# Record tables of a graph kernel with their rows permuted inside each batch of 512, so that a partition's four records lie side by side

## The chip, the cores and the metric

The kernel runs on one core of a Trainium2 chip. The metric is the device time of one launch in microseconds (us), the median of three timed runs. A profile is taken in an execution of its own, beside the timed ones; its span is the time from its first instruction to its last.

## The reference, cut to what matters

Four graph layers, each followed by a mixture-of-experts layer, work on a table `x` of 3125 nodes by 256 features and one list of 50000 edges (`src`, `dst`, attributes per edge). What the change touches is how an edge's data are found. Each graph layer has the form of layer 0:

```python
h = x @ W_in2f                                   # nodes
Wij = ssp(rbf @ Wf1 + bf1) @ Wf2 + bf2           # rbf: 64 attributes per edge
Wij = Wij * dist_cut                             # one weight per edge
x_ij = h[idx_j] * Wij                            # row of the node at the far end
m = jax.ops.segment_sum(x_ij, idx_i, num_segments=n_atoms)   # sum at the near end
m = ssp(m @ Wo1 + bo1) @ Wo2 + bo2
return x + m
```

Layer 0 sums at `src`; layers 1 to 3 sum at `dst`. Layer 1 uses 16 attributes per edge and an attention with a softmax over a node's edges, layer 2 no attributes, layer 3 128 attributes and an attention.

## The kernel before

Nodes stand in 25 tiles of 128. So that a sum over a node's edges becomes a matmul with a 0/1 matrix, the kernel first sorts the edges. Every edge gets a slot number; slots are grouped in pairs of tiles (256 slots) that hold edges of one node tile only, and there are 440 tiles of 128 slots (220 pairs). Two tables in device memory hold one record per slot: `records_by_src` (68 numbers, 272 bytes: the 64 attributes of layer 0 and four numbers of placement) and `records_by_dst` (148 numbers, 592 bytes: 128 and 16 attributes and four of placement). `META` is the number of placement columns: a weight, the far node, the near node inside its tile, and a one. A slot without an edge keeps a blank record, whose near node is -1.

**l0n**, the first stage, makes both. Three things run beside each other.

- *The src numbers.* `CellNumbering` (from L524) sorts by src, which is unsorted. The edges stand in a [128, 391] grid; 390 full columns go in 30 groups of 13. For a group, VectorE makes 0/1 tiles (`hot_group`, L653), TensorE counts with them (L818, L820) and VectorE picks each edge's own count out (`take_group`, one instruction per column, L726). Then `put_group` (L738) casts the 13 columns to integers into `to.pos` and raises `pos_ready`. The odd column 391 is cast at L749. After the groups VectorE computes the pairs' tables (25 instructions at L765).
- *The dst numbers.* `Numbering.vector` (L437 to L517) sorts by dst in one go over all 391 columns, also on VectorE, after the node tiles' part of l0n. `pos` is cast at L494; the pairs' tables follow, to the stage's last VectorE instruction, L517.
- *The src scatter.* `Scatter` (from L825) runs on Pool. A ring of record buffers is filled by the SyncE queue from the attributes; `copy` (L872) waits until the group's numbers are out (`placed`, L870), then copies placement and numbers; `scatter` sends one indirect DMA per column (L890), 128 records each to the rows that `pos` names. `scatter_left` does the last columns from `to.pos` itself (L925). The dst table is scattered by the same class in the stage l0e.

The edge stages **l0e** (by src), **l1e** and **l3e** (by dst) each run 110 batches of 512 slots, four tiles of 128. For a batch, the SyncE queue loads the records (`load_batch`, L1105), VectorE casts the far nodes (`find`, L1143), Pool gathers four times 128 rows of the node table (L1121), and the other engines compute and sum. Five record buffers form a ring; `rec_free` lets a buffer be loaded again. Between l0e and l1e, a stage called the means loads 20 numbers (80 bytes) of the dst records, and l1e loads the last four (16 bytes).

`batch_records` gives the view of a batch in the table. Slot number and table row were the same, so slot `t * 128 + p` of a batch lay `t * 128 + p` rows behind the batch's first: a partition p of the record tile took four pieces, one per tile t, 128 rows apart. For a batch that is 512 pieces.

Of the kernel before, what the change touches and what calls it, by code (L numbers as in the profile page):

```python
# [8 lines left out]
I32 = mybir.dt.int32  # L9
# [3 lines left out]
ALU = mybir.AluOpType  # L13
# [3 lines left out]
P = 128  # L17
# [7 lines left out]
EC = E // P  # L25
# [3 lines left out]
BATCH = 4  # L29
# [26 lines left out]
def at(tensor, t, width):  # L56

    if isinstance(t, int):
        return tensor[:, t * width:(t + 1) * width]
    return tensor[:, bass.ds(t * width, width)]  # L60
# [106 lines left out]
def row(vector):  # L167

    return vector.rearrange("(o n) -> o n", o=1)


def column(vector):

    return vector.rearrange("(p o) -> p o", o=1)


def spread(vector):

    return row(vector).to_broadcast([P, vector.shape[0]])
# [7 lines left out]
def tiled(ap, width):  # L187
    return ap.rearrange("p (t d) -> p t d", d=width)
# [210 lines left out]
class Numbering:  # L399
# [37 lines left out]
    def vector(self, dve, net):  # L437
        to, near, far = self.to, self.near, self.far
        t = {n: (v if n == "ps" else v[:, :]) for n, v in self.t.items()}
        part, blk, counted = t["part"], t["blk"], self.t["counted"]  # L440
        match = [t[f"match{k}"] for k in range(UN)]
        link = Chain(dve, self.chain)
# [36 lines left out]
        with dve.Fori(0, NI) as i:  # L479
# [3 lines left out]
            for k in range(UN):  # L483
                b = i * UN + k
# [6 lines left out]
            dve.wait_ge(self.pos_step, base3 + 3 * UN)  # L491
        link(dve.tensor_tensor(pos[0], pos[0], pos[1], ALU.add))
        link(dve.tensor_copy(to.pos[:, :], pos[0]))

        m = to.meta[:, :].rearrange("p (j r) -> p j r", r=META)
        link(dve.memset(to.meta[:, :], 1.0))
# [27 lines left out]
class CellNumbering:  # L524
# [13 lines left out]
    def __init__(self, s, net, shared, to, near, far, weight, spare, turned_into):  # L538
# [23 lines left out]
        self.hot = [s.sb(f"cell_hot{b}", [P, self.COLUMNS * KEYS], BF16) for b in range(2)]  # L562
        self.posf = [s.sb(f"cell_posf{b}", [P, self.COLUMNS]) for b in range(2)]
        self.posf_left = s.sb("cell_posf_left", [P, 1])
        self.picked = [s.sb(f"cell_picked{b}", [P, KEYS]) for b in range(4)]
        self.of_column = s.sb("cell_of_column", [self.ROWS, self.PARTS * CELLS], BF16)
        self.upto_column = s.sb("cell_upto_column", [self.ROWS, self.PARTS * CELLS])
# [89 lines left out]
    def vector(self, dve, net):  # L657
        t, to, near, far = self.t, self.to, self.near, self.far
        key, a_i, b_i = self.key, t["part"], self.part_b
        link = Chain(dve, self.chain)  # L660
# [72 lines left out]
        def put_group(g, b):  # L733
            dve.wait_ge(self.taken, (g + 1) * self.COLUMNS // 2 + 2)
            if (g + 1) * self.COLUMNS % 2:
                dve.wait_ge(self.odd_taken, g // 2 + 1)
            dve.sem_inc(self.tick, 1)
            dve.tensor_copy(at(to.pos, g, self.COLUMNS), self.posf[b][:, :]).then_inc(self.pos_ready, 1)  # L738

        take_group(0, 0)  # L740
        put_group(0, 0)
        for g in range(1, self.GROUPS):
            if g + 1 < self.GROUPS:
                self.hot_group(dve, g + 1, (g + 1) % 2)
            take_group(g, g % 2)
            put_group(g, g % 2)
        link(dve.tensor_tensor_reduce(self.picked[0][:, 0:CELLS], self.hot_left[:, 0:CELLS], self.upto_left[:, :], 1.0, 0.0,
                                      ALU.mult, ALU.add, self.posf_left[:, :]))
        dve.tensor_copy(to.pos[:, EC:EC + 1], self.posf_left[:, :]).then_inc(self.pos_ready, 1)  # L749

        link(dve.memset(self.end[:, NT - 1:NT], float(PAIRS * PAIR - 1)))
        link(dve.tensor_scalar(self.end[:, 0:NT - 1], self.first[:, 1:NT], float(PAIR), -1.0, ALU.mult, ALU.add))
# [192 lines left out]
def batch_records(records, q, lo, hi):  # L945

    rows = records[bass.ds(q * (BATCH * P), BATCH * P), :]
    return rows.rearrange("(t p) r -> p t r", p=P)[:, :, lo:hi]


def l0_gnn_nodes(net):
# [128 lines left out]
class Gather:  # L1080
# [21 lines left out]

    def load_batch(self, sp, q, b):
        sp.wait_ge(self.rec_free, q + 1)
        sp.dma_start(tiled(self.rec[b][:, :], self.n), batch_records(self.placed.records, q, self.lo, self.placed.width))\  # L1105
            .then_inc(self.rec_loaded[b], 16)

    def load(self, sp, more=None):
# [1929 lines left out]
def combine_and_means(net, name, to):  # L3038
# [13 lines left out]
    with ExitStack() as ctx:  # L3052
# [58 lines left out]
        @block.sync  # L3111
        def _(sp):
            def load(q, i, b):
                sp.wait_ge(rest_ready, q + 1)
                sp.dma_start(tiled(rec[b][:, :], n), batch_records(placed.records, q, lo, placed.width))\
                    .then_inc(loaded[b], 16)

            def put(q, i, b):
                sp.wait_ge(kept, RING + q + 1)
                sp.dma_start(net.attr_parts[bass.ds(q * P, P), :], partsT[b][:, :]).then_inc(stored[b], 16)  # L3120

            skewed(sp, (0, by_five(load)), (9, put), ring=DEEP)
            for b in range(DEEP):
                sp.wait_ge(stored[b], NB // DEEP * 16)
# [1311 lines left out]
```

## Time and profile before

| what | us |
|---|---|
| median of the timed runs | 6331.62 |
| the timed runs | 6319.6 to 6334.9 |
| the profiled execution: its span | 7197.4 |
| l0n in it: from 15.8 to | 832 |
| l0e: to | 1957 |
| means | 2541 to 2761 |
| l1e | 2878 to 3994 |
| l3e | 5993 to 6817 |

The stage limits are the first and last instructions of a stage's lines in the trace. The profiled execution is not one of the timed runs; its span stands beside their median because every duration of a single instruction comes from it.

### The profile page before, as it was taken

How to read it: one execution, taken by the hardware profiler on the slowest of the kernel's cores; microseconds unless marked ns; L12 is line 12 of the kernel's file. 1: busy time of each engine (PE TensorE's matmuls, PEld its weight loads, DVE VectorE, ACT ScalarE, POOL GpSimd, SP SyncE). 2: the span in 40 equal slices, each digit the busy share in tenths (PEclk: the TensorE clock that was granted, in tenths of full speed). 3: DMA queues.
4: the chain of work that ended last, by engine and by line, in shares of the span. 5: the costliest groups of instructions: out<-in, count | busy, mean ns of one | idle time of the engine just before them, and what ended most of it. 6: DMA issues, size and time to landing. Idle time of an engine off the chain costs nothing. (4 is left out here: it accounts for less than half of the span.)

```text
span 7197.4 us, 118819 instructions
## 1 busy us (share of the span) xinstructions
PE 5162.2 (72%) x25594; PEld 3845.3 (53%) x25595; DVE 4306.9 (60%) x13225; ACT 2821.1 (39%) x8212; POOL 3018.8 (42%) x3493
## 2 busy tenths in 40 slices
PE   3333377787745657788888399969999996767686
PEld 2222255555533425566666366655657774655575
DVE  4334655666536757799999677773433335655622
ACT  0000255565521143567676311113633333655522
POOL 4665155555444630788888022213310003555421
PEclk9999688888866857899999599989999997777788
DMA  6411133333324752222223255644420003444443
GB/s 215 152 44 38 47 91 88 90 92 95 82 71 139 215 130 63 67 69 67 69 67 67 68 170 182 188 144 136 148 70 9 13 8 100 120 106 110 93 148 124
DMA packets 787071, 719.50 MB, mean 100 GB/s; under 512 B 349384, under 2 KB 692974, under 8 KB 786383
## 3 DMA queue, kind: packets, MB, share of 16 engines
q1 hardware_dynamic: 596344, 372.06, 18.4%
q0 software_dynamic: 120064, 280.26, 14.5%
q10 hardware_dynamic: 70486, 65.22, 2.6%
q8 instruction: 63, 1.03, 0.1%
q14 instruction: 114, 0.93, 0.0%
HBM read 520.74 MB, written 201.60 MB: 100 GB/s over the span
## 5 line engine op out<-in xcount | busy, mean ns | idle before, releaser
L1121 POOL DMA_INDIRECT l3e_rows<-table,l3e_idx x440 | 425.9, 968 | 961.4 <-DVE l3e_idx L1143 600.7
L1121 POOL DMA_INDIRECT l0e_rows<-table,l0e_idx x440 | 425.5, 967 | 580.8 <-DVE l0e_idx L1143 438.6
L1121 POOL DMA_INDIRECT l1e_rows<-table,l1e_idx x440 | 429.6, 976 | 121.4 <-issue 121.4
L3470 ACT ACTIVATE l1e_weighted<-l1e_rows,l1e_power 128x64 f32<-128x64 f32 x1760 | 463.0, 334 | 14.7 <-ACT l1e_power L3461 7.3
L1411 PE MATMUL l0e_ps_w<-l0e_wf,l0e_hidT 128*128 128x256 f32 x1760 | 461.7, 421 | 0.0
L1411 PEld LDWEIGHTS l0e_ps_w<-l0e_wf,l0e_hidT 128*128 128x128 f32 x1760 | 363.4, 212 | 163.7 <-issue 109.3
L890 POOL DMA_INDIRECT records_by_src<-l0n_rec_src,l0n_pos_at_src x390 | 376.3, 965 | 119.2 <-issue 112.3
L818 PE MATMUL l0n_cell_ps<-l0n_cell_hot,l0n_cell_before 128*128 128x175 bf16 x390 | 133.4, 342 | 406.5 <-issue 233.7
L3425 PE MATMUL l3e_ps_s<-l3e_weighted,l3e_onehot 128*128 128x257 f32 x880 | 301.6, 499 | 132.8 <-ACT l3e_weighted L3472 84.6
L3411 PE MATMUL l1e_ps_row<-net_ident,l1e_logit 128*128 128x128 f32 x1760 | 277.7, 281 | 127.1 <-DVE l1e_logit L3606 126.2
L726 DVE CUSTOM_DVE_ANT_0 l0n_cell_picked<-l0n_cell_hot,l0n_cell_ps 128x175 f32<-128x175 bf16 x390 | 114.6, 333 | 394.1 <-remote 310.2
L1402 PE MATMUL l0e_ps_h<-l0e_rbfT,l0e_wf 64*128 64x512 f32 x440 | 163.6, 805 | 256.2 <-ACT l0e_rbfT L1438 195.7
L2144 ACT ACTIVATE l2fe_hT<-l2fe_ps_h,l2fe_own,l2fe_own 128x320 f32<-128x320 f32 x320 | 197.4, 617 | 310.8 <-PE l2fe_ps_h L2094 310.5
L2777 ACT ACTIVATE l1fg_hT<-l1fg_ps_h,l1fg_b_cols 128x256 f32<-128x256 f32 x256 | 107.3, 470 | 530.4 <-PE l1fg_ps_h L2720 511.2
L3425 PEld LDWEIGHTS l3e_ps_s<-l3e_weighted,l3e_onehot 128*128 128x128 f32 x880 | 202.3, 247 | 206.7 <-ACT l3e_weighted L3472 105.5
L3601 POOL TENSOR_TENSOR l1e_e<-l1e_e,l1x_att 128x512 f32<-128x512 f32 x220 | 274.4, 1269 | 89.4 <-DVE l1e_e L3584 53.0
L3411 PEld LDWEIGHTS l1e_ps_row<-net_ident,l1e_logit 128*128 128x128 f32 x1760 | 192.9, 138 | 207.5 <-issue 154.4
L3999 PE MATMUL l2d_ps<-l2d_wide,net_work 128*128 128x512 f32 (+2 forms) x800 | 292.0, 521 | 8.2 <-DVE l2d_wide L4050 5.9
L818 PEld LDWEIGHTS l0n_cell_ps<-l0n_cell_hot,l0n_cell_before 128*128 128x128 bf16 x390 | 50.9, 131 | 450.0 <-issue 252.0
L3328 DVE TENSOR_REDUCE l1e_tile_top<-l1e_ps_row 128x2 f32<-128x512 f32 x440 | 287.7, 684 | 5.8 <-PE l1e_ps_row L3414 4.5
L1343 DVE SCALAR_TENSOR_TENSOR l0e_hidT<-l0e_ps_h,l0e_bf_low,l0e_raised 128x512 f32<-128x512 f32 x220 | 154.9, 746 | 220.9 <-ACT l0e_raised L1457 177.3
L2197 DVE SCALAR_TENSOR_TENSOR net_x<-l2fe_ps_y,l2fe_mix,net_x 128x256 f32 x200 | 96.7, 484 | 309.4 <-PE l2fe_ps_y L2106 309.4
(843 smaller groups left out, 15399.4 us busy)
## 6 DMA issues: line engine op xcount, KB each, us to landing
counts<-l1f_total ACTq DMA_DIRECT2D x272, 128.0 KB
l1fg_w_in<-in_L_ffn_W SPq DMA_DIRECT2D x32, 1024.0 KB
l1fg_w_out<-in_L_ffn_W SPq DMA_DIRECT2D x32, 1024.0 KB
records_by_dst<-l0n_blank_dst SPq DMA_DIRECT2D x5, 6512.0 KB
l3e_rec<-records_by_dst SPq DMA_DIRECT2D x110, 296.0 KB
l2d_counts<-counts SPq DMA_DIRECT2D x208, 128.0 KB, 2.4
l2d_counts<-counts POOLq DMA_DIRECT2D x192, 128.0 KB
l3fg_w_in<-in_L_ffn_w SPq DMA_DIRECT2D x16, 1024.0 KB
```

The source lines that it names most:

```text
L818: pe.matmul(out, self.before[:, :], self.hot[g % 2][:, c * KEYS:c * KEYS + CELLS], start=True, stop=False)
L890: pool.indirect_dma_start(self.to.records, bass.IndirectOffsetOnAxis(self.pos_at[b][:, j:j + 1], 0), at(self.rec[b], j, self.to.width), No ...
L1121: pool.indirect_dma_start(at(self.rows[b], k, self.width), None, self.table, bass.IndirectOffsetOnAxis(self.idx[b][:, k:k + 1], 0)).then_i ...
L1402: pe.matmul(ps_h[:, c, :], wf1[half, :], rbfT[b][half, :], start=True, stop=True).then_inc(hidden, 1)
L1411: ins = pe.matmul(ps_w[:, k, m * D:(m + 1) * D], hidT[b][:, c * WIDE + (2 * k + m) * P:c * WIDE + (2 * k + m + 1) * P], at(wf2, c, D), sta ...
L2144: act.activation(hT[l][:, m * GROUP + half * PART:m * GROUP + (half + 1) * PART], ps_h[:, c % 4, 0:PART], func, bias=own[l][0][:, m:m + 1] ...
L3328: dve.tensor_reduce(tile_top[:, c:c + w], tiled(ps_row[:, side, 0:w * PAIR], PAIR), AX.X, ALU.max)\
L3411: pe.matmul(ps_row[:, side, lo:lo + P], logit[b][:, c:c + 1].to_broadcast([P, P]), net.ident[:, :], is_transpose=True, start=h == h0 and m ...
L3425: ins = pe.matmul(ps_s[:, k, 0:W], at(g.onehot[b], m, P), at(weighted, m, W), start=m == 2 * k, stop=m > 2 * k)
L3470: act.activation(out[:, h, 0:each], g.rows[b][:, lo:lo + each], ACT.Copy, scale=power[b][:, m * heads + h:m * heads + h + 1])
L3601: pool.tensor_tensor(e, e, self.att[:, :].unsqueeze(1).to_broadcast([P, 2, D]), ALU.mult).then_inc(self.times_att, 1)
L3999: ins = pe.matmul(ps[0:k_in, n % 2, 0:width(g)], lhsT, wide[k % WIDE][:, 0:width(g)], start=t == 0, stop=False)
```

## The change

The row of a slot in both record tables is permuted inside each batch of 512 slots. With slot = 512 q + 128 t + p, the row was 512 q + 128 t + p and becomes 512 q + 4 p + t. The four records of partition p are then four rows that follow each other. The slot itself, so the tile and the partition in which an edge is processed, stays.

- `batch_records` reads the new order; where all columns are loaded (l0e by src, l3e by dst, `lo == 0`) a partition takes one piece: 1088 bytes for src, 2368 for dst, 128 pieces a batch. Where only the last columns are loaded (means, l1e) there are still 512 pieces.
- `row_of_slot` is new: eight integer instructions on VectorE, each waiting for the one before, that turn a slot's number into its row. It is called on the 13 columns of each group in `put_group`, on the odd column, and once on the dst table's 391 columns. In `put_group` the cast before it is now waited for as well. After the odd column a wait for all of the row numbers is added.
- Two new tiles, `cell_low` and `cell_high`, [128, 13]; the dst table uses tiles that are there.

```diff
 class Numbering, vector:
+        self.other = self.t["match0"][:, :].bitcast(I32)
         ...
         link(dve.tensor_tensor(pos[0], pos[0], pos[1], ALU.add))
         link(dve.tensor_copy(to.pos[:, :], pos[0]))
+        link(row_of_slot(dve, link, to.pos[:, :], part, self.other))

 class CellNumbering, __init__:
+        self.low = s.sb("cell_low", [P, self.COLUMNS], I32)
+        self.high = s.sb("cell_high", [P, self.COLUMNS], I32)
 put_group:
             dve.sem_inc(self.tick, 1)
-            dve.tensor_copy(at(to.pos, g, self.COLUMNS), self.posf[b][:, :]).then_inc(self.pos_ready, 1)
+            slot = at(to.pos, g, self.COLUMNS)
+            link(dve.tensor_copy(slot, self.posf[b][:, :]))
+            row_of_slot(dve, link, slot, self.low[:, :], self.high[:, :]).then_inc(self.pos_ready, 1)
 the odd column:
-        dve.tensor_copy(to.pos[:, EC:EC + 1], self.posf_left[:, :]).then_inc(self.pos_ready, 1)
+        link(dve.tensor_copy(to.pos[:, EC:EC + 1], self.posf_left[:, :]))
+        row_of_slot(dve, link, to.pos[:, EC:EC + 1], self.low[:, 0:1], self.high[:, 0:1]).then_inc(self.pos_ready, 1)
+        dve.wait_ge(self.pos_ready, self.GROUPS + 1)
+        dve.sem_inc(self.tick, 1)

 def batch_records(records, q, lo, hi):
     rows = records[bass.ds(q * (BATCH * P), BATCH * P), :]
-    return rows.rearrange("(t p) r -> p t r", p=P)[:, :, lo:hi]
+    if (lo, hi) == (0, records.shape[1]):
+        return rows.rearrange("(p t) r -> p (t r)", p=P)
+    return rows.rearrange("(p t) r -> p t r", p=P)[:, :, lo:hi]
+
+def row_of_slot(dve, link, slot, low, high):
+    link(dve.tensor_single_scalar(low, slot, P - 1, op=ALU.bitwise_and))
+    link(dve.tensor_single_scalar(low, low, 2, op=ALU.logical_shift_left))
+    link(dve.tensor_single_scalar(high, slot, 7, op=ALU.logical_shift_right))
+    link(dve.tensor_single_scalar(high, high, BATCH - 1, op=ALU.bitwise_and))
+    link(dve.tensor_tensor(low, low, high, ALU.bitwise_or))
+    link(dve.tensor_single_scalar(high, slot, 9, op=ALU.logical_shift_right))
+    link(dve.tensor_single_scalar(high, high, 9, op=ALU.logical_shift_left))
+    return dve.tensor_tensor(slot, low, high, ALU.bitwise_or)

 Gather.load_batch:
         sp.wait_ge(self.rec_free, q + 1)
-        sp.dma_start(tiled(self.rec[b][:, :], self.n), batch_records(self.placed.records, q, self.lo, self.placed.width))\
+        rec = self.rec[b][:, :] if self.lo == 0 else tiled(self.rec[b][:, :], self.n)
+        sp.dma_start(rec, batch_records(self.placed.records, q, self.lo, self.placed.width))\
             .then_inc(self.rec_loaded[b], 16)
```

## Rows read from the trace of the kernel before

**Rows 1.** The page's head: span and instructions.
```profile
span 7197.4 us, 118819 instructions
```

**Rows 2.** Waits by ended idle time, 0 to 840: total us, count, longest us.
```profile
DVE l0n_cell_picked L726 <- remote: 310.2, 51, 11.3
POOL l0n_rec_src L872 <- DVE l_pos_src L738: 152.5, 14, 55.9
```

**Rows 3.** Timeline, l0n: start, us, engine, line, operation; in brackets idle and releaser.
```profile
304.63 0.35 PE L820 MATMUL l0n_cell_ps<-l0n_cell_upto_low,l0n_cell_ident 65*128 65x175 bf16 x1
313.76 0.34 DVE L726 CUSTOM_DVE_ANT_0 l0n_cell_picked<-l0n_cell_hot,l0n_cell_ps 128x175 f32<-128x175 bf16 x1 [9.90 <-remote]
```

**Rows 4.** Timeline, VectorE in l0n.
```profile
66.62 2.36 DVE L653 TENSOR_SCALAR l0n_cell_hot<-l0n_cell_key_row,l0n_cell_key 128x176 bf16<-128x176 bf16 x13
74.73 2.40 DVE L653 TENSOR_SCALAR l0n_cell_hot<-l0n_cell_key_row,l0n_cell_key 128x176 bf16<-128x176 bf16 x13
...
652.23 0.17 DVE L738 CAST l_pos_src<-l0n_cell_posf 128x13 int32<-128x13 f32 x1
...
830.91 0.39 DVE L517 TENSOR_TENSOR net_keep_dst<-l0n_pair_blk 128x219 f32<-128x219 f32 x1
```

**Rows 5.** Timeline, l0e around 1410 (SPq is SyncE's DMA queue).
```profile
1407.72 1.19 ACT L1438 ACTIVATE l0e_rbfT<-l0e_ps_t 64x512 f32<-64x512 f32 x2 [3.65 <-DMA records_by_src<-l0n_rec_src,l0n_pos_at_src]
...
1418.77 0.38 SPq L1105 DMA_DIRECT2D l0e_rec<-records_by_src  x1
1420.09 0.16 DVE L1143 CAST l0e_idx<-l0e_rec 128x4 int32<-128x4 f32 x1
...
1427.80 0.16 DVE L1143 CAST l0e_idx<-l0e_rec 128x4 int32<-128x4 f32 x1
```

**Rows 6.** Stretches: length, busy PE PEld DVE ACT POOL, clock, DMA share, GB/s.
```profile
832.00:1957.00 1125.00, 855.02 (x3524) 617.19 (x3524) 673.32 (x1327) 648.40 (x1431) 606.90 (x616) 0.86 0.35 89
...
5992.00:6818.00 826.00, 577.37 (x2860) 464.04 (x2860) 496.14 (x2425) 462.92 (x1541) 425.90 (x440) 0.77 0.45 111
```

**Rows 7.** Timeline, l3e around 6400.
```profile
6400.45 0.37 SPq L1105 DMA_DIRECT2D l3e_rec<-records_by_dst  x1
6405.19 0.16 DVE L1143 CAST l3e_idx<-l3e_rec 128x4 int32<-128x4 f32 x1
...
6409.99 0.16 DVE L1143 CAST l3e_idx<-l3e_rec 128x4 int32<-128x4 f32 x1
```

**Rows 8.** Pool in l0n, and VectorE beside it: timeline, and L890 grouped.
```profile
75.00 0.25 POOL L872 COPY l0n_rec_src<-l_meta_src 128x52 f32<-128x52 f32 x1 [55.92 <-DVE l_pos_src L738]
...
686.70 0.91 POOL L925 DMA_INDIRECT records_by_src<-l0n_rec_src,l_pos_src  x1 [0.55 <-POOL l0n_rec_src L919]
...
L890 POOL DMA_INDIRECT records_by_src<-l0n_rec_src,l0n_pos_at_src x390: 954/958/1192, 76.4 to 681.9; - x195
...
656.08 12.05 DVE L765 SCALAR_TENSOR_TENSOR l0n_pair_blk<-l0n_pair_no,l0n_cell_first,l0n_pair_blk 128x220 f32<-128x220 f32 x25
662.00 1.15 POOL L890 DMA_INDIRECT records_by_src<-l0n_rec_src,l0n_pos_at_src  x1 [0.30 <-issue]
```

**Rows 9.** DMA: queue (packets, MB, share) 900:1900, 6000:6800; one load's landing.
```profile
q1 hardware_dynamic: 96960, 25.74, 12.3%
...
q1 hardware_dynamic: 55440, 31.83, 15.6%
...
l2d_counts<-counts SPq DMA_DIRECT2D x208, 128.0 KB, 2.4
```

**Rows 10.** Timeline, VectorE's integer and wide instructions near the end of l0n.
```profile
829.09 0.18 DVE L513 TENSOR_SCALAR net_round_word_dst<-net_round_word_dst 128x44 int32<-128x44 int32 x1
829.31 0.24 DVE L514 TENSOR_TENSOR net_round_word_dst<-net_round_word_dst,net_block_row_dst 128x44 int32<-128x44 int32 x1
...
810.41 0.57 DVE L492 TENSOR_TENSOR l0n_pos_a<-l0n_pos_a,l0n_pos_b 128x391 f32<-128x391 f32 x1 [0.21 <-DVE l0n_pos_a L490]
```

**Rows 11.** Waits, 840 to 1960: total us, count, longest us.
```profile
POOL l0e_rows L1121 <- DVE l0e_idx L1143: 438.6, 66, 156.4
```

## The prediction

> **What bounds the kernel now.** I read the page first: its chain of work names only the last few instructions, so it doesn't say what bounds 7197.4 us [rows 1], and the kernel has to be read stage by stage. The second thing to see stands in the times: the profiled execution's own span is 7197.4 us, the timed runs have a median of 6331.6 us. The profiled execution is 866 us longer than the thing that I have to predict, and before any wait is believed it must be known which idle time belongs to the profiled execution alone.
>
> The three stages that the change touches show it. In l0n (both tables' row numbers are computed, and the src table is scattered) the waits show VectorE idle for 310.2 us in 51 pieces with no releaser that the profile knows ("remote") [rows 2]. One of them: the matmul that VectorE waits for ends at 304.63 + 0.35 = 304.98, VectorE starts at 313.76 [rows 3], while the usual round of 13 columns takes 74.73 - 66.62 = 8.11 us altogether [rows 4]. In l0e, ScalarE idles 3.65 us before its copy and the row names as releaser a scatter of the stage before, long over [rows 5]. An undisturbed batch there takes 1427.80 - 1420.09 = 7.71 us, 110 of them 848 us; the stage has 1125 us [rows 5, 6]: 277 too many. In l3e a batch takes 6409.99 - 6405.19 = 4.80 us, 110 of them 528 us, the stage has 826 us [rows 6, 7]: 298 too many.
>
> What l0n would be without those stalls: VectorE's first row numbers are out at about 75 (Pool's copy of them starts at 75.00 [rows 8]); 29 further groups at 8.11 make 235, so 310; from its last group to its last instruction it took 830.91 + 0.39 - 652.23 = 179 us [rows 4], so it would end at 489. Pool ends its scatter at 686.70 + 0.91 = 687.6 [rows 8]; of its waits for row numbers, 152.5 us in all, only the first, 55.9 us, is before the loop [rows 2], so 96.6 go with VectorE's stalls and it would end at 591. In the profiled execution VectorE ends l0n; without the stalls Pool does, and the stage shrinks by 831 - 591 = 240. The three together: 240 + 277 + 298 = 815 us, of the 866 us that the timed runs lack. So I take it that the timed runs have next to none of these stalls, that Pool's chain of indirect DMAs sets the end of l0n with VectorE about 100 us ahead of it, and that l0e and l3e run at the pace of their undisturbed batches.
>
> A rule speaks against that. The Trainium skill (Runtime: NRT & Kernel Launch, The ~15µs preamble/postamble breakdown) says that a profile's total exceeds the executed time by a gap of about 6.2 us, the same for every kernel. By that rule the stalls would be in the timed runs too. Here the difference is 866 us [rows 1], so the trace and the times don't agree with it; what it would do here is the first rival below.
>
> **The change, part by part.** *The record loads, l0e and l3e.* Each of the 2 x 110 loads becomes 128 pieces instead of 512, with the same bytes. In l0e the hardware queue's packets took 12.3% of 16 engines x 1000 us over 96960 packets, 20 ns each (a mix of 272 B and others); in l3e 15.6% x 16 x 800 us / 55440 = 36 ns for 592 B [rows 9]. One engine has 32 pieces of a load: 0.65 us and 1.15 us. A piece four times as long costs between one old piece and four: the load saves 0 to 0.49 us in l0e, 0 to 0.86 us in l3e, at the engine. Who gets it? A load is issued when a batch's records are released, three steps behind, for the batch five further on, so it is needed at the second find after it. l0e: issued 1418.77, needed 1427.80, 9.0 us. l3e: issued 6400.45, needed 6409.99, 9.5 us [rows 5, 7]. A 128 KB load from the same queue lands in 2.4 us [rows 9]; for l0e's 136 KB that is near; for l3e's 296 KB, by bytes, at most 5.6 us (an estimate from that row). Both are in time with 3.9 us or more to spare, so the gain is hidden: 0. If that cover were gone, it is the second rival.
>
> *The narrow loads (means, l1e).* They still have 512 pieces of 80 and 16 bytes, from other addresses. Nothing in the rows tells their cost apart; I take 0, either sign, a few us.
>
> *Eight integer instructions after each group's row numbers (l0n, src table).* A shift of 44 columns takes 0.18 us and the next instruction of the chain starts 0.22 us after it, a two-input one takes 0.24 [rows 10]; the group's own 13-column cast takes 0.17 [rows 4]. Six at 0.22 and two at 0.28 are 1.9 us a group. Thirty groups are 57 us, the odd column 1.5 us. *The dst table's eight instructions over 391 columns:* the nearest row is 0.57 us [rows 10], so at most 8 x 0.6 = 4.8 us. Together 63 us on VectorE. A group then takes 10.0 us; Pool needs (591 - 75) / 30 = 17 us for one and stays behind. VectorE ends at 489 + 63 = 552, Pool at 591: 39 us remain, hidden. If the cover is gone, it costs 63.
>
> *The first group's row numbers.* Nothing hides these: Pool's first copy waits 55.92 us for them [rows 8] and everything on Pool follows. +1.9 us on the path. Between 0 and 1.9 if the blank rows were late too; I take 1.9.
>
> *Pool beside VectorE's new instructions.* While VectorE runs 25 two-input instructions back to back [rows 8] (12.05 us), Pool's indirect DMA takes 1.15 us instead of its median 0.958: 0.19 more in each 1.45. For 1.9 us of new instructions a group that makes 0.25 us, for 30 groups 7.5 us at most, on Pool, which ends the stage; 0 at least, since six of the eight have one input. I take 3.
>
> The Trainium skill (SBUF — State Buffer, Who interferes with whom) says that VectorE and GpSimd share a port pair as an exclusive lock, so that the second to come is blocked completely for the other's whole instruction. By that Pool would lose up to all of the 59 us of new instructions in the loop; the rows show a fifth of an instruction's time, so by rows it is 3.
>
> *The last wait* (the row numbers' count after the odd column) stops VectorE for one cast's latency, some 0.2 us; behind it are only the instructions that are hidden with it.
>
> *Order of edges:* a slot keeps its tile and partition, so every matmul and segment sees the same data; the scatters write as many rows. 0.
>
> **The sum.** +1.9 + 3 = +5 us on 6331.6: **6336.5 us**, +0.08%. Within 0.3% (19 us, about what a measurement of this kernel can tell from no change).
>
> **The rivals.** *VectorE ends l0n (slower).* If the stalls are in the timed runs as well, VectorE is last in l0n by 831 - 688 = 143 us and the 63 us lie bare: 6331.6 + 63 = 6395. It decides from the point where the stalls that the timed runs keep are over some 59 us of the 310 (39 us of slack, of which Pool keeps pace with 31%). For it: the profile as it stands; 815 is not all of 866, and the undisturbed paces come from single batches. Against it: the 866. The skill's rule on the gap leads here. 0.14.
>
> *The port lock (slower).* Pool is held for the whole of each new instruction: 59 us, 6390. Against it the 1.15 us rows. 0.04.
>
> *The loads are on the path (faster).* Pool waits 438.6 us in l0e for the index cast that needs a load [rows 11]; were that the load and not the stalls, the pieces' time comes back, up to (0.49 + 0.86) x 110 = 148 us, half of it as the middle: 6258. Against it: 9 us between issue and need. 0.09.
>
> *A smaller gain from fewer packets beside the row gathers* over 19 us: 0.03.
>
> *The change doesn't make one piece of a row* (pieces stay short): nothing on the path depends on it, so the time is as forecast.
>
> **How the numbers follow.** Forecast 0.70: 6336.5, with 6318 to 6352 for the unknown small costs and the runs' own spread (6319.6 to 6334.9). Slower 0.14 + 0.04, near 6390 to 6395. Faster 0.09 + 0.03. The range reaches to the slower cases, which hold more: 6314 to 6396, leaving out 0.12.
>
> **What the next profile would show.** The hardware queue's packets fall by 384 a batch in l0e and l3e; the loads land sooner and no stage's undisturbed batch (7.7 and 4.8 us) gets shorter. Pool's first copy starts near 77. VectorE's last l0n instruction comes up to 63 us later. The stalls may move with the number of packets or instructions, so the profiled span can change by more than the median, in either direction, and is not the test. The forecast is wrong if the median moves by over 19 us; up by about 60, VectorE ends l0n outside the profiler as well; down, some load was waited for.

## The result, and the profile after

The kernel after takes 6345.25 us (median of 7 runs, 6342.79 to 6349.78), the kernel before 6326.72 us beside it (7 runs, 6319.6 to 6334.9). The ratio is 1.0024, with an interval of 1.0015 to 1.0034: 9 to 22 us slower. That is within the 0.3% that the prediction called no change, and inside its range, but it is not nothing, and the predicted +5 us lies below the interval. The median moved by 18.5 us, just short of the 19 us at which the prediction called itself wrong. Where the rest comes from is what the runs had to settle. Of the 33 timed runs of the kernel before beside some of the later runs one took 10191.02 us and is in no ratio, so executions far too long occur outside the first profile as well.

The profiled execution of the kernel after was undisturbed. That of the kernel before, from which the prediction was made, was not, so the kernel before was profiled a second time (the first experiment below). The stages are compared with that second profile; each length is from the start of the first instruction on a stage's tiles to the start of the last:

| stage | before, second profile (us) | after (us) |
|---|---|---|
| l0n | 591.7 | 589.3 |
| l0e | 841.6 | 835.6 |
| means | 172.6 | 181.4 |
| l1e | 1115.1 | 1112.0 |
| l3e | 601.6 | 601.5 |
| span | 6340.2 | 6343.6 |

One stage is longer: the means, which the prediction had passed over with "0, either sign, a few us". The waits of that stage, first in the second profile of before, then after (engine, tile and line, what it waited for: us in all, times, longest):

```profile
ACT means_parts L3160 <- DMA means_rec<-records_by_dst: 12.3, 3, 10.7
DVE means_onehot L1076 <- DMA means_rec<-records_by_dst: 2.6, 2, 2.0
```

```profile
ACT means_parts L3184 <- DMA means_rec<-records_by_dst: 30.9, 45, 11.0
DVE means_onehot L1099 <- DMA means_rec<-records_by_dst: 28.0, 50, 2.3
```

Two engines that waited for a record load only at the stage's start (3 and 2 times) now do so in nearly every second batch (45 and 50 of 110). The loads are the narrow ones, 80 bytes a slot, that the change leaves at 512 pieces. What they wait for is the issue of the load and not its landing, as the paired stores below show. The tile's own view gives the time that the SyncE queue needs to issue one such load (min/median/max in ns, first and last start), before and after:

```profile
L3115 SPq DMA_DIRECT2D means_rec<-records_by_dst x28: 382/383/389, 2060.5 to 2099.0; - x28
```

```profile
L3139 SPq DMA_DIRECT2D means_rec<-records_by_dst x26: 567/567/582, 2060.6 to 2098.9; - x26
```

The same bytes in the same number of pieces take 184 ns more to issue. The Trainium skill (Perfetto Trace Analysis, DMA Instruction — HWDGE (DVE, Sync)) says that the span shown for such an instruction runs until all of the transfer's descriptors are generated, and that the queue is free for its next instruction only then. The rows of the queue agree: the next issue never starts inside the span of one. Timeline of the queue, before (a load and a store of results per batch), then after:

```profile
2076.15 0.38 SPq L3115 DMA_DIRECT2D means_rec<-records_by_dst  x1
2076.79 0.36 SPq L3120 DMA_DIRECT2D attr_parts<-means_partsT  x1
2077.41 0.38 SPq L3115 DMA_DIRECT2D means_rec<-records_by_dst  x1
```

```profile
2087.03 0.57 SPq L3139 DMA_DIRECT2D means_rec<-records_by_dst  x1
2087.90 0.35 SPq L3144 DMA_DIRECT2D attr_parts<-means_partsT  x1
2088.52 0.57 SPq L3139 DMA_DIRECT2D means_rec<-records_by_dst  x1
```

A batch costs the queue 2077.41 - 2076.15 = 1.26 us before and 2088.52 - 2087.03 = 1.49 us after. The stage itself needs some 1.42 us a batch before (30 batches from 2061.70 to 2104.19, by the starts of their first VectorE instruction). So the queue had 0.16 us to spare in such a batch, and the change takes 0.23, most of it in the load (the store's median goes from 357 to 394 ns). Two batches in ten take the queue longer than that in both kernels: in the kernel after, loads start at 2083.46, 2085.37, 2087.03 and 2088.52, which is 1.91 and 1.66 us before it is 1.49 again. With them the queue's mean is some 1.55 us a batch after the change, and the spare time before it was less than 0.16.

In the rest, the change did what it says. The hardware queue in 700 us of l0e and in 500 us of l3e (packets, MB, share of 16 engines), before, then after:

```profile
q1 hardware_dynamic: 91452, 24.28, 16.0%
...
q1 hardware_dynamic: 51216, 29.41, 21.5%
```

```profile
q1 hardware_dynamic: 55344, 24.38, 13.3%
...
q1 hardware_dynamic: 13904, 29.29, 18.9%
```

Over the whole execution the queue's packets go from 596344 to 511864, which is 84480 or 220 loads times 384. The loads land sooner (median in l3e, 3.4 us before and 3.0 after; in l0e 2.6 and 2.3, read from the count that the data engines raise), and l3e is not shorter. That l0e is 6 us shorter can't be put down to them: in the runs below whose l0e is that of the kernel before it takes 837.0 to 842.4 us, and the run with doubled loads shows what sets its length.

### The profile page after: what moved, and what is told of

Its sections match the earlier page's. It is cut to its first block and busy times, and to the rows that moved or that the text cites. A ratio compares the mean times of both kernels' runs of the same rounds, so it can differ in the third digit from the quotient of the medians.

```text
span 6343.6 us, 119012 instructions
## 1 busy us (share of the span) xinstructions
PE 4937.5 (78%) x25530; PEld 3709.8 (58%) x25595; DVE 4351.6 (69%) x13481; ACT 2811.1 (44%) x8212; POOL 3080.0 (49%) x3493
## 3 DMA queue, kind: packets, MB, share of 16 engines
q1 hardware_dynamic: 511864, 372.06, 20.1%
## 5 line engine op out<-in xcount | busy, mean ns | idle before, releaser
L1145 POOL DMA_INDIRECT l0e_rows<-table,l0e_idx x440 | 447.4, 1017 | 149.9 <-issue 131.9
L3494 ACT ACTIVATE l1e_weighted<-l1e_rows,l1e_power 128x64 f32<-128x64 f32 x1760 | 463.0, 334 | 14.7 <-ACT l1e_power L3485 7.3
L899 POOL DMA_INDIRECT records_by_src<-l0n_rec_src,l0n_pos_at_src x390 | 396.6, 1017 | 115.5 <-issue 109.5
L1435 PE MATMUL l0e_ps_w<-l0e_wf,l0e_hidT 128*128 128x256 f32 x1760 | 411.6, 387 | 32.4 <-DVE l0e_shifted L1376 32.4
L1435 PEld LDWEIGHTS l0e_ps_w<-l0e_wf,l0e_hidT 128*128 128x128 f32 x1760 | 327.3, 191 | 158.4 <-issue 85.4
L3449 PE MATMUL l3e_ps_s<-l3e_weighted,l3e_onehot 128*128 128x257 f32 x880 | 247.2, 425 | 95.9 <-ACT l3e_weighted L3496 95.9
L2916 POOL DMA_INDIRECT outputs<-l1fg_y,l1fg_target x64 | 69.9, 1092 | 467.6 <-DVE l1fg_y L2853 456.0
L2744 PE MATMUL l1fg_ps_h<-l1fg_xT,l1fg_w_in 128*128 128x256 f32 x1024 | 264.6, 381 | 1.7 <-DVE l1fg_xT L2841 0.8
L3593 PE MATMUL l1e_ps_x<-l1x_xr,l1e_nodehot 128*128 x880 | 255.6, 392 | 2.7 <-ACT l1e_nodehot L3477 2.7
L3449 PEld LDWEIGHTS l3e_ps_s<-l3e_weighted,l3e_onehot 128*128 128x128 f32 x880 | 160.6, 202 | 163.1 <-ACT l3e_weighted L3496 146.9
L3941 POOL DMA_DIRECT2D l2d_counts<-counts x192 | 107.2, 559 | 285.1 <-ACT l2d_wide L4133 139.4
```

The costliest lines, as they stand in the source:

```text
L899: pool.indirect_dma_start(self.to.records, bass.IndirectOffsetOnAxis(self.pos_at[b][:, j:j + 1], 0), at(self.rec[b], j, self.to.width), No ...
L1145: pool.indirect_dma_start(at(self.rows[b], k, self.width), None, self.table, bass.IndirectOffsetOnAxis(self.idx[b][:, k:k + 1], 0)).then_i ...
L1435: ins = pe.matmul(ps_w[:, k, m * D:(m + 1) * D], hidT[b][:, c * WIDE + (2 * k + m) * P:c * WIDE + (2 * k + m + 1) * P], at(wf2, c, D), sta ...
L2744: ins = pe.matmul(ps_h[:, n % HALVES, (m % 2) * SLICE:(m % 2 + 1) * SLICE], w_in[b][:, c * F + m * P:c * F + (m + 1) * P], at(xT[b], c, SL ...
L3449: ins = pe.matmul(ps_s[:, k, 0:W], at(g.onehot[b], m, P), at(weighted, m, W), start=m == 2 * k, stop=m > 2 * k)
L3494: act.activation(out[:, h, 0:each], g.rows[b][:, lo:lo + each], ACT.Copy, scale=power[b][:, m * heads + h:m * heads + h + 1])
```

## The experiments

**The kernel before, once more.** Not changed at all.

> The kernel before, unchanged, profiled a second time. If the stalls of the first profile (310 us in l0n, some 280 in l0e and 300 in l3e) belong to that one profiled execution, the span now comes out near the timed 6327 us and the three stages at about 590, 835 and 600 us as in the kernel after. If they belong to this kernel under the profiler (its many short load pieces), the span is again near 7200 us.

```profile
span 6340.2 us, 118755 instructions
```

The stalls are gone, and the span stands beside the timed runs. They belonged to that one execution, not to what the kernel does every time and not to its short pieces; what caused them is not known. This is the ground on which everything else is compared.

**The loads alone.**

```
-    return rows.rearrange("(t p) r -> p t r", p=P)[:, :, lo:hi]
+    if (lo, hi) == (0, records.shape[1]):
+        return rows.rearrange("(p t) r -> p (t r)", p=P)
+    return rows.rearrange("(p t) r -> p t r", p=P)[:, :, lo:hi]
```

> Only the loads are changed (one long piece a partition, and the narrow ones from the new addresses); the rows of the tables are not permuted, so an edge comes out at another tile and partition and the sums are over other edges. Theory A (the 18.5 us come from the new instructions in l0n and what they do to Pool): 6325 to 6329 us, no change. Theory B (they come from the stages that read the tables, means and l1e with their short pieces from other addresses among them): 6337 to 6345 us. If long pieces gain anything that the numbers then take away: below 6317 us.

Measured: 6347.77 us, ratio 1.0017 (1.0008 to 1.0026). The means take 180.5 us, and their waits are those of the kernel after:

```profile
ACT means_parts L3163 <- DMA means_rec<-records_by_dst: 29.6, 39, 11.1
DVE means_onehot L1078 <- DMA means_rec<-records_by_dst: 24.8, 45, 2.5
```

**The instructions alone.** `row_of_slot` at every place, its constants changed so that a slot keeps its number:

```
-    link(dve.tensor_single_scalar(low, low, 2, op=ALU.logical_shift_left))
+    link(dve.tensor_single_scalar(low, low, 0, op=ALU.logical_shift_left))
...
-    link(dve.tensor_single_scalar(high, high, BATCH - 1, op=ALU.bitwise_and))
+    link(dve.tensor_single_scalar(high, high, 0, op=ALU.bitwise_and))
...
-    link(dve.tensor_single_scalar(high, slot, 9, op=ALU.logical_shift_right))
-    link(dve.tensor_single_scalar(high, high, 9, op=ALU.logical_shift_left))
+    link(dve.tensor_single_scalar(high, slot, 7, op=ALU.logical_shift_right))
+    link(dve.tensor_single_scalar(high, high, 7, op=ALU.logical_shift_left))
```

> All eight instructions at each of their places, with other constants so that a slot keeps its own number; old loads. Theory A: 6341 to 6347 us, nearly the whole 18.5. Theory B: 6329 to 6333 us, the 1.6 us by which Pool starts later in l0n and little else.

Measured: 6341.65 us, ratio 1.0005 (0.9996 to 1.0014); means 171.4, l0n 589.8. No change that can be told. The expectations of these runs were written in us against the 6326.72 us of the result; beside these runs the kernel before took 6337.62 us, so the ratios have to be held against them. Theory A wanted 1.0023 to 1.0032 here and no change from the loads, theory B 1.0004 to 1.0010 here and 1.0016 to 1.0029 from the loads. Both ratios are theory B's: the loss comes with the loads.

**Five instructions instead of eight.**

```
-    link(dve.tensor_single_scalar(low, slot, P - 1, op=ALU.bitwise_and))
-    link(dve.tensor_single_scalar(low, low, 2, op=ALU.logical_shift_left))
+    link(dve.tensor_scalar(low, slot, P - 1, 2, ALU.bitwise_and, ALU.logical_shift_left))
...
```

> The kernel after with the row number in five instructions instead of eight (two operations in one where both take a constant). Theory A: three eighths of the cost go, 6337 to 6339 us. Theory B: 0.6 us go, 6344 to 6346 us.

Measured: 6349.27 us, ratio 1.0020 (1.0011 to 1.0029), means 181.4. As ratios theory A wanted 1.0016 to 1.0019 and theory B 1.0027 to 1.0030; the interval holds the one and most of the other, so the time doesn't decide. The means do: with three eighths of the instructions gone they are as long as in the kernel after.

**Only the src table permuted.** The dst table, which the means read, keeps its rows; the src numbers and the long load of l0e stay.

```
-    if (lo, hi) == (0, records.shape[1]):
+    if records.shape[1] == 64 + META:
         return rows.rearrange("(p t) r -> p (t r)", p=P)
-    return rows.rearrange("(p t) r -> p t r", p=P)[:, :, lo:hi]
+    return rows.rearrange("(t p) r -> p t r", p=P)[:, :, lo:hi]
```

> Only the src table is permuted, with its eight instructions and its long load; the dst table keeps the old rows and the old loads in means, l1e and l3e. Theory P (the loss is the SyncE queue's issue of the narrow loads in means, 567 ns instead of 383): means back at 171 to 173 us (after: 181), whole kernel within 3 us of the kernel before, ratio 0.9995 to 1.0005. Rival N (a good part of the loss comes from the instructions in l0n, 5 to 8 us): ratio 1.0008 to 1.0013 although means is back.

Measured: 6336.23 us, ratio 1.0004 (0.9995 to 1.0014), means 170.1 us, issues of 383 ns again. Both the means' loss and its cause go with the dst table's rows. (The ratio falls in theory P's range, but all of rival N's, 1.0008 to 1.0013, lies inside the interval, here and in the run of the instructions alone. What speaks against N is the stage: with the instructions l0n takes 592.0 us here, 589.8 in the run of the instructions alone, and 591.7 in the kernel before.)

**Is it the issue, or the landing?** A load that is issued more slowly also lands later (2.36 us after its start instead of 2.10), and that alone could have set the pace of the five buffers. Two kernels separate the two: the results of two batches go out in one transfer, so that SyncE has half of the stores less to issue, in the kernel before and in the kernel after.

```
+                if b % 2:
                     sp.wait_ge(kept, RING + q + 1)
-                    sp.dma_start(net.attr_parts[bass.ds(q * P, P), :], partsT[b][:, :]).then_inc(stored[b], 16)
+                    sp.dma_start(net.attr_parts[bass.ds((q - 1) * P, 2 * P), :].rearrange("(n p) w -> p n w", n=2),
+                                 tiled(parts_two[b // 2][:, :], BATCH * P)).then_inc(stored[b // 2], 16)
```

> The kernel before, with two batches of the means' results stored by one transfer, so that SyncE issues 1.5 instead of 2 transfers a batch. In the kernel before SyncE's issues take some 1.27 us of the 1.42 us that a batch takes in means, so theory P says that VectorE and not SyncE sets the pace there: means 168 to 173 us, ratio 0.999 to 1.0003. If SyncE set the pace in the kernel before already: means 145 to 160 us, ratio 0.9955 to 0.998.

> The kernel after with the same paired stores. Theory P: SyncE has 0.35 us a batch less to do, the slower issue of the narrow load no longer sets the pace, means 170 to 175 us, ratio 0.9995 to 1.001. Rival L (the narrow loads land later, 2.36 instead of 2.10 us, and the buffers' ring makes that the pace): means stays at 179 to 183 us, ratio 1.0015 to 1.0025.

Measured: before with pairs 6338.95 us, ratio 1.0005 (0.9996 to 1.0014), means 171.7 us. After with pairs 6338.06 us, ratio 1.0006 (0.9997 to 1.0015), means 169.1 us. The kernel after with pairs, the load's issue and the waits of the means:

```profile
L3140 SPq DMA_DIRECT2D means_rec<-records_by_dst x29: 542/561/572, 2060.3 to 2099.7; - x29
...
ACT means_parts L3187 <- DMA means_rec<-records_by_dst: 12.3, 4, 11.1
DVE means_onehot L1099 <- DMA means_rec<-records_by_dst: 2.7, 2, 2.5
```

The issue is as slow as in the kernel after and the load lands no sooner (2.46 us), yet the waits are gone and the stage is as short as in the kernel before. So it is SyncE's share of a batch that costs the time, not the landing; rival L falls. In the kernel before the same relief gains nothing, so there SyncE was not the limit: VectorE is busy there for 39.96 of 42.49 us, here in stretches of 30 batches each (length, busy PE PEld DVE ACT POOL, clock, DMA share, GB/s), before and after:

```profile
2061.70:2104.19 42.49, 30.19 (x243) 17.89 (x240) 39.96 (x115) 31.97 (x91) 0.00 (x0) 0.50 0.55 122
```

```profile
2057.93:2104.33 46.40, 30.23 (x240) 17.91 (x240) 40.69 (x115) 33.40 (x91) 0.00 (x0) 0.50 0.50 112
```

The bound passes from VectorE (1.42 us a batch) to SyncE (46.40 / 30 = 1.55).

**Waits on SyncE.** Meant to slow the queue without touching a load:

```
+                for _ in range(4):
                     sp.wait_ge(rest_ready, q + 1)
```

> The kernel before, in means with three more waits on a semaphore that is there already ahead of every narrow load, on the SyncE queue alone; loads and rows as before. Theory P: once SyncE's part of a batch passes 1.42 us, the stage grows by 110 times what is above it; if a wait takes 0.06 us or more, means is at 176 to 195 us with issues of 383 ns and landings of 2.1 us. Rival L: means stays at 171 to 174 us, since the landing is as before.

Measured: 6332.35 us, ratio 0.9993 (0.9983 to 1.0002), means 170.5 us. The three waits turned out too cheap to decide anything: 1.39 - 1.26 = 0.13 us together, 0.04 each, where the expectation wanted 0.06. Queue timeline:

```profile
2070.91 0.38 SPq L3116 DMA_DIRECT2D means_rec<-records_by_dst  x1
...
2072.30 0.38 SPq L3116 DMA_DIRECT2D means_rec<-records_by_dst  x1
```

A batch takes SyncE 1.39 us, just under the stage's 1.42. This fits theory P and doesn't exclude L.

**Why is the issue slower?** The narrow load of the means was cut into two transfers of two tiles each, with the old and with the new rows:

```
+                rows = batch_records(placed.records, q, lo, placed.width)
+                for h in (slice(0, 2), slice(2, 4)):
-                sp.dma_start(tiled(rec[b][:, :], n), batch_records(placed.records, q, lo, placed.width))\
-                    .then_inc(loaded[b], 16)
+                    sp.dma_start(tiled(rec[b][:, :], n)[:, h, :], rows[:, h, :]).then_inc(loaded[b], 16)
```

> The kernel before, with the narrow load of means in two transfers of two tiles each; old rows. Gives the issue time of a transfer of 2 x 128 pieces where the pieces of one partition lie 128 rows apart: expected 0.33 to 0.39 us. SyncE then has about 1.9 us of work a batch and sets the pace: means 215 to 240 us.

> The kernel after with the same two transfers; new rows, so the pieces of one partition lie one row apart, but two of every four rows are skipped and the rows no longer form one even sequence of 512. If the slow issue (567 ns) comes from such an even sequence meeting a tile of 4 x 128 pieces: 0.33 to 0.39 us an issue, as in the kernel before. If it comes from neighbouring rows going to one partition: 0.45 us or more, and means 10 us or more longer than with the old rows.

The issues, old rows, then new rows:

```profile
L3117 SPq DMA_DIRECT2D means_rec<-records_by_dst x43: 372/373/373, 2060.1 to 2099.3; - x43
```

```profile
L3141 SPq DMA_DIRECT2D means_rec<-records_by_dst x43: 372/373/373, 2059.8 to 2099.1; - x43
```

373 ns both, and means 215.4 and 216.2 us, since SyncE now issues three transfers a batch. Half as many pieces are issued only 10 ns faster than all of them with the old rows (383), so the number of pieces is not what costs. Nor is it that neighbouring rows go to one partition: that holds for the halves with the new rows too. What is left is the form of the whole load: with all four tiles, the 512 rows are one sequence of equal steps of 592 bytes, on the other side stand 128 partitions of four pieces, and with the old rows both sides are 128 by 4. The l1e loads have that form and show the same (378 ns before, 553 after); with some 10 us a batch l1e has room for it and is no longer. How the transfer's addresses are written down inside the instruction is not in the trace, so that the mismatch of the two forms is the reason is the reading that is left, not shown.

The whole-kernel times of these two, 6374.84 and 6390.41 us, are single runs and are not compared.

**Do the long pieces gain anything that is hidden?** In l0e and l3e of the kernel before, each batch's records are loaded once more into a tile that nobody reads, ahead of the load that is used.

```
+        if self.lo == 0:
+            sp.wait_ge(self.spare_loaded, q * 16 + 16)
+            sp.dma_start(tiled(self.spare[:, :], self.n), batch_records(self.placed.records, q, self.lo, self.placed.width))\
+                .then_inc(self.spare_loaded, 16)
         sp.dma_start(tiled(self.rec[b][:, :], self.n), batch_records(self.placed.records, q, self.lo, self.placed.width))\
             .then_inc(self.rec_loaded[b], 16)
```

> The kernel before; in l0e and l3e every batch's records are loaded a first time into a tile that nobody reads, on the same queue right ahead of the load that is used, which so lands later by the issue and the pieces of one load (about 1.0 us in l0e, 1.5 us in l3e). If the loads have the slack of the prediction (needed 9 us after the issue): l0e 838 to 845, l3e 599 to 608 us, ratio 0.9995 to 1.0015. If the loads are on the path, and long pieces had so been worth something: 110 times 1.0 and 1.5 us, up to 275 us more, ratio 1.02 to 1.045.

Measured: 6329.91 us, ratio 0.9991 (0.9981 to 1.0000). The used load landed 0.4 us later in l0e (3.0 us) and 0.7 us later in l3e (4.1), less than expected, but more than the long pieces gain (0.3 and 0.4 us), and the kernel as a whole lost nothing: that the loads are on the path all along, with up to 275 us to lose, falls. Both stages left what was expected, l0e 826.3 us (15 shorter), l3e 617.2 us (16 longer), in the one profile that there is. In l3e the data engines are busy for 0.77 of the time instead of 0.62:

```profile
612.00:1438.00 826.00, 782.56 (x3524) 581.86 (x3524) 668.36 (x1327) 644.43 (x1430) 617.36 (x616) 0.98 0.57 140
5342.00:5959.00 617.00, 481.76 (x2860) 388.44 (x2860) 489.13 (x2425) 461.07 (x1541) 435.97 (x440) 0.93 0.77 202
```

In l3e the later load was not free. VectorE waits for it there (waits from 5342 to 5959), as it never does in l3e of the kernel before or after:

```profile
DVE l3e_idx L1152 <- DMA l3e_rec<-records_by_dst: 25.4, 6, 14.7
```

The 14.7 us are one wait near the stage's end, for a load that landed 23.7 us after its issue, and nearly as long as what the stage grew by; the others above 1 us stand at the stage's start and 20 us before that one. So this run doesn't show that l3e bears a later load for free. That the pieces' time is hidden there rests on the kernel after, where the loads land 0.4 us sooner and l3e is as long as before.

In l0e it is Pool that sets the length. In the kernel before (second profile) it waits for the index cast, which needs the load, three times, one of them 16.1 us, at the stage's start:

```profile
POOL l0e_rows L1121 <- DVE l0e_idx L1143: 16.7, 3, 16.1
```

In each of the thirteen profiles without the stalls l0e takes 208 to 210 us more than Pool is busy in it (842.0 and 632.7 us in the kernel before, 836.1 and 628.1 after, 826.8 and 617.4 here, to the end of the last instruction). All through the stage Pool goes from one transfer to the next, 0.3 us apart. The 15 us that l0e lost here are Pool's own: 78 of its 616 transfers took over 1.1 us, against 128 in the kernel before. Why fewer of them did is open. The records' loads, but for the stage's first, are off that path, in this run as in the others.

**Where the cover of VectorE's instructions ends.** The eight instructions three times over, with the constants of the run of the instructions alone.

```
 def row_of_slot(dve, link, slot, low, high):
+    for n in range(3):
...
```

> The eight instructions three times over at each place, with the constants that leave a slot's number as it is; old loads. VectorE ended l0n at 478 us in the kernel before and at 545 us with the instructions once, Pool at 605 us in both. If Pool sets the end until VectorE is later than it: VectorE at 478 + 3 x 67 = 679 us now ends the stage, l0n 70 to 80 us longer, ratio 1.010 to 1.013. If the instructions were partly on the path already: more than 80 us. If VectorE's work is off the path in the timed runs altogether: within 10 us.

Measured: 6395.10 us, ratio 1.0094 (1.0077 to 1.0110), l0n 654.4 us: 63 us longer, less than the 70 to 80 expected. Last instruction of VectorE and last transfer of Pool in l0n:

```profile
670.18 0.39 DVE L519 TENSOR_TENSOR net_keep_dst<-l0n_pair_blk 128x219 f32<-128x219 f32 x1
...
590.71 1.32 POOL L934 DMA_INDIRECT records_by_src<-l0n_rec_src,l_pos_src  x1 [0.28 <-POOL l0n_rec_src L928]
```

VectorE, 8 us earlier than expected, now ends the stage, 79 us after Pool, and 60 us of it are in the timed runs. So VectorE's instructions in l0n cost nothing until VectorE is later than Pool, and all of it from there on.

## Why the prediction was right, and where it was wrong

**The stalls are the profiled execution's own.** Right, and shown: without any change the second profile is 857 us shorter. The rule of a fixed gap, which the prediction held against its trace, was not tested by it: the 866 us lie between two executions, and where one execution has both figures they agree (the second profile's own device time is 6341.88 us, its span 6340.2). The working had one bad piece. The undisturbed batch of l3e, 4.80 us [rows 7], was one of the shortest: without stalls the stage takes 602 us, not 528, so of the 298 us charged to stalls only 223 were. For l0e (848 worked out, 841.6 seen) the single batch was a fair one. A pace from one batch needs a second one from elsewhere in the stage.

**Pool ends l0n, VectorE about 100 us ahead.** Right, and shown. The kernel before, second profile, then after: Pool's first copy, VectorE's last instruction, Pool's last transfer.

```profile
74.97 0.25 POOL L872 COPY l0n_rec_src<-l_meta_src 128x52 f32<-128x52 f32 x1 [55.92 <-DVE l_pos_src L738]
...
477.94 0.39 DVE L517 TENSOR_TENSOR net_keep_dst<-l0n_pair_blk 128x219 f32<-128x219 f32 x1
...
607.49 0.92 POOL L925 DMA_INDIRECT records_by_src<-l0n_rec_src,l_pos_src  x1 [0.55 <-POOL l0n_rec_src L919]
```

```profile
76.62 0.26 POOL L881 COPY l0n_rec_src<-l_meta_src 128x52 f32<-128x52 f32 x1 [57.57 <-DVE l_pos_src L971]
...
543.78 0.39 DVE L519 TENSOR_TENSOR net_keep_dst<-l0n_pair_blk 128x219 f32<-128x219 f32 x1
...
605.09 0.91 POOL L934 DMA_INDIRECT records_by_src<-l0n_rec_src,l_pos_src  x1 [0.55 <-POOL l0n_rec_src L928]
```

VectorE ends at 478 (489 worked out) and with the change at 544: 66 us later, where the sum had 63. Pool ends at 608, not 591. Its 390 transfers of L890 take 399.8 us together, 376.3 in the stalled profile, which more than covers the 17 us. The cause is to be seen beside VectorE's wide two-input instructions of the dst numbers, which in the stalled profile ran when Pool was nearly through; beside them Pool's transfers take far longer than the 1.15 us of [rows 8], as here in the kernel after:

```profile
452.77 4.42 DVE L459 TENSOR_TENSOR_SCAN l0n_counted<-l0n_one_row,l0n_match 128x391 f32 x5
...
452.99 1.52 POOL L899 DMA_INDIRECT records_by_src<-l0n_rec_src,l0n_pos_at_src  x1 [0.30 <-issue]
```

With the instructions three times over, where the scans come later, fewer of Pool's transfers meet them, and Pool is through at 592. So the first rival's point of decision lay further off than worked out: 608 - 478 = 130 us of slack before, and 62 us after. (By the prediction's own figures it lay at 39 / 0.69 = 57 us of stalls, not 59.)

**The terms of the sum.** The first group's numbers were to cost 1.9 us on the path: Pool's first copy is 76.62 - 74.97 = 1.65 us later, but l0n doesn't end later, since what Pool meets of VectorE's wide instructions shifts by more than that: the same 390 transfers take 396.6 us, 3.2 less. Pool beside the new instructions was to lose 3 us: it loses nothing, its transfer beside one of them takes what it takes alone:

```profile
300.37 0.39 DVE L969 TENSOR_SCALAR l0n_cell_high<-l_pos_src 128x13 int32<-128x13 int32 x1
...
299.83 0.96 POOL L899 DMA_INDIRECT records_by_src<-l0n_rec_src,l0n_pos_at_src  x1 [0.30 <-issue]
```

The port lock, the second rival, by which Pool would be held, falls with the same row, and with all 69 transfers of l0n that overlap the groups' new instructions: the longest took 0.98 us. There is a hold, but VectorE bears it, where there is slack: its shift in this row took 0.39 us, its neighbours 0.17. Of the 248 such instructions 37 were lengthened so, to 0.43 us at most, and each of the 37 ended 23 to 25 ns before the end of a Pool transfer. The long loads were to gain nothing since they are hidden: right, by the paths of l0e and l3e above.

**The step that failed** is the term of the narrow loads: "nothing in the rows tells their cost apart; I take 0, either sign, a few us". It cost some 10 us, all in the means: the six kernels with issues of 383 ns and stores one by one, the stalled profile left aside, have means of 170.1 to 172.6 us (mean 170.9), the three with 567 ns 180.5 to 181.4 (mean 181.1). The step weighed the pieces on the data engines, and there nothing changed. It did not look at the queue that issues them. The trace of before couldn't give the new issue time, but it did show how much a batch of the means could bear: 1.26 us of issues in a stage that needs 1.42. With that the term would have had a price for every size: next to nothing up to 0.16 us an issue, 110 times whatever is above it, so 110 x (0.23 - 0.16) = 8 us for what was measured, near the 10 seen. The range held since other costs had widened it, not because this one was in it, and that the kernel got slower, as the +5 us said, was luck: none of the 5 us was found where the sum had them.

**What stays open.** The 10 us of the means are 0.16%, which lies inside the measured 0.24% (0.15 to 0.34). The other 0.08% no stage shows; the kernel after with paired stores, in which the means are healed, stands at 1.0006 (0.9997 to 1.0015), just as the kernel before with paired stores (1.0005). Whether a few us remain beside the means can't be told from these runs. Why the issue is slower is argued from the forms of the transfers and not shown.

## What to carry to other kernels

A transfer has a price on the queue that issues it, apart from its bytes and pieces, and a loop whose queue is nearly full pays for it: count the issues of a batch against the stage's time for a batch, and look at each transfer whose address form a change touches, the ones that it isn't about above all. Laying a table out for one wide load changes the form of every narrow load from it. And before a wait in a profile is believed, hold the profiled span against the timed runs: here 12% of it was no part of the kernel's usual time.

## What the runs showed of the hardware

The issue of a load of 512 pieces took 383 ns with rows in four runs of 128 and 567 ns (16-byte pieces: 378 and 553) with the same rows as one even sequence; 256 pieces took 373 ns either way, a load of 128 long pieces 333. Pool's indirect transfer, 0.96 us alone, took 1.42 to 1.52 us beside VectorE's scans over 391 columns and 0.96 us beside integer instructions over 13 columns; of those, 37 that fell into the end of a transfer lasted until 23 to 25 ns before that end, 0.43 us at most, the others mostly 0.17.
